# Order of the three part products, and VectorE's low parts of h one slot later, in a fused attention and expert layer

## The chip, the cores and the metric

One core of a Trainium2 chip runs the whole program. The metric is the device time of one execution in microseconds, lower is better. TensorE is called PE in the rows, its weight loads PEld, VectorE is DVE, ScalarE is ACT, GpSimd is POOL, and SyncE, whose queue issues the transfers, is SP.

## The reference

The input is 4 batches of 1024 tokens with 128 features. After a layer norm without weights, two branches run on the same tokens: 16-head attention with its own layer norm, and a mixture of 8 experts with a hidden size of 512, of which the best 2 are weighed per token. The result is the input plus attention times silu(experts).

```python
x = L0_attn_z
xn = _layernorm(x, axis=-1)
s = _L0_attn_ref(xn, ...)            # softmax(q k / sqrt(8)) v, 16 heads of 8, then W_proj
g = _silu(_L0_ffn_ref(xn, ...))
x = x + s * g

# in _L0_ffn_ref: all 8 experts are computed for every token
h = gelu(einsum('td,edh->eth', xf, W1) + b1[:, None, :], approximate=False)
expert_out = einsum('eth,ehd->etd', h, W2) + b2[:, None, :]
out = einsum('etd,te->td', expert_out, weights)
```

## The kernel before

The 4096 tokens are cut into NG = 8 groups of 512. The program has two stages. In the **expert stage** each group passes through HT = 32 chunks: 8 experts times 4 chunks of 128 hidden features. In the **attention stage** that follows, 32 pairs of heads are worked off in 256 blocks. The change touches only the expert stage.

**Products in parts.** A product in full fp32 costs several passes on TensorE, so most are made from rounded parts in fp32r. A weight matrix w is held as a high part (`w1h`, `w2h`, tile `w_hi`) and a low part (`w1l`, `w2l`, tile `w_lo`); the activations likewise: `xh`, `xl` (tiles `xn_t_hi`, `xn_t_lo`) and `hh`, `hl` (tiles `h_hi`, `h_lo`). `up(i)` makes the hidden chunk i from three products into one PSUM bank: L947 high by high, L948 low weights by high x, L949 high weights by low x. `down(i)` adds the chunk into the expert's output by three products as well: L968 and L969 with `hh`, and L971 with `hl`. Every fourth chunk (i = 3 mod 4) is not split and goes through L963 in fp32. Each product loads its own weights (a PEld row beside the PE row).

**Who makes h.** ScalarE takes the bank of `up(i)` twice through gelu: L823 writes the rounded `hh`, L826 the full `h_split` (`h32`). The low part is `h_split - h_hi`. VectorE makes it for the first chunk of each expert (i = 0 mod 4, `by_vector`, line L1272), GpSimd for the next two (L685). `down(i)` waits for it in `hl_done`, just ahead of L971.

**The order.** Every engine works off a plan of slots, one slot per chunk, that is written out by hand; `run_slots` calls the steps of slot 0, 1, 2, ... in order. Within a slot of group g stand first what is left of the experts of group g-1, then the extras, then the preparation of group g+1 (`pre`: statistics, router, q, k and v), then the experts of group g. TensorE runs `up(i)` in slot i and `down(i)` in slot i+3. The extras are the **early row maxima** for the attention stage: TensorE's product L985 writes one of two banks in turn, VectorE's L1336 reduces it. Product m waits until maximum m-2 is done, because it writes the same bank (`early_scores`, `pe.wait_ge(S("R"), m - 1)`). There are 256 of them, 27 in each 32 slots, so some slots hold two.

**VectorE's queue is strictly in order.** In slot i it holds, as far as present: the maxima, the preparation step, `low_h(i)` or `combine(e)` (L1289, in slots 4e+7). Its low part begins with `wait(dve, "h32", ...)`, and everything behind it on VectorE stands until ScalarE has written `h_split`.

## Time and profile before

| | us |
|---|---|
| median of 3 runs | 1103.75 (1102.54 to 1105.91) |
| the profiled execution | 1103.0 |
| its span, first to last instruction | 1101.2 |
| of this the expert stage | to about 512 |
| of this the attention stage | from about 512 |

The profiled execution is 0.75 us below the median; 1.8 us of it lie outside the span. In the steady part of the expert stage one group of 512 tokens takes about 62 us: VectorE's first low part of a group starts at 272.53, 334.80, 396.56 and 457.72 us. In the 60 us from 300 to 360 us TensorE is busy for 58.33 us, VectorE for 47.66, ScalarE for 41.42, GpSimd for 39.09, at the full TensorE clock (2.4 GHz).

A matmul's row is longer than the time that it holds up the next one: its end is modelled. An fp32r product of 512 columns is shown with 0.39 us, while the next one starts 0.23 us later. So a wait of TensorE costs the time between two starts minus 0.23 us, which is 0.16 us more than the idle time that is shown in brackets behind the row.

### The profile page before, as it was taken

The page shows a single profiled execution, that of the slowest core. Times are in us where ns is not written, and L with a number is a line of the kernel's source. Part 1 is how long each engine was busy: PE and PEld are TensorE (multiplying, and loading weights), DVE is VectorE, ACT ScalarE, POOL GpSimd, SP SyncE. Part 2 cuts the span into 40 slices and gives each one's busy share as a digit, 9 for nine tenths or more (in the row PEclk, how much of TensorE's full clock was granted, in tenths as well). Part 3 has the DMA queues.
Part 4 walks back from the last instruction along what each step waited for, and adds up shares of the span by engine and source line. Part 5 has one row for each costly group of instructions (what it writes and reads, how often), then busy time and mean ns, then how long its engine had stood idle before and what let it go on. Part 6 is the DMA issues. An engine that isn't in the chain of part 4 may idle for free.

```text
span 1101.2 us, 17451 instructions
## 1 busy us (share of the span) xinstructions
PE 1029.3 (93%) x5865; PEld 444.1 (40%) x5897; DVE 883.7 (80%) x1589; ACT 866.9 (79%) x1190; POOL 368.0 (33%) x555
## 2 busy tenths in 40 slices
PE   4998999999999999999999999999999999999997
PEld 3675666666666666664222222122222121122222
DVE  5647877787878787765999899989998998899943
ACT  6876667676767677666898998989898989798985
POOL 4786656657666667554001000001000001000010
PEclk9999999999999999999999999999999999999998
DMA  6432221414142232324212221212112221122102
GB/s 183 123 99 68 66 83 31 120 30 121 31 107 50 64 80 51 97 51 120 51 44 53 55 53 39 68 40 54 42 52 51 56 53 42 51 53 54 25 24 82
DMA packets 99410, 72.02 MB, mean 65 GB/s; under 512 B 21693, under 2 KB 83834, under 8 KB 99322
## 3 DMA queue, kind: packets, MB, share of 16 engines
q1 hardware_dynamic: 99322, 70.92, 24.5%
q8 instruction: 47, 0.77, 0.3%
q14 instruction: 41, 0.34, 0.1%
HBM read 53.12 MB, written 15.46 MB: 62 GB/s over the span
## 4 chain that ended last, share of the span: by engine, by line
PE 34%; ACT 8%; DVE 7%; issue 2%; SPq 1%; DMA 0%; POOL 0%; ACTq 0%; DVEq 0%; POOLq 0%
PE psum L1055 17%; PE psum L1034 8%; ACT p_ring L869 8%; PE psum L999 7%; DVE neg_max_half L1318 7%; PE psum L1084 1%; ACT o_sb L860 1%; DMA den<-o_sb 0%; SPq L469 0%; PE psum L1098 0%; PE psum L1010 0%; SPq L473 0%; DVE neg_max_rest L1327 0%; DVE y L1379 0%; POOL h_lo L685 0%
## 5 line engine op out<-in xcount | busy, mean ns | idle before, releaser
L869 ACT ACTIVATE p_ring<-psum 128x1024 f32<-128x1024 f32 x512 | 494.8, 1026 | 59.7 <-PE psum L1034 54.3
L1318 DVE TENSOR_REDUCE neg_max_half<-psum 128x1 f32<-128x512 f32 x768 | 481.6, 681 | 44.5 <-PE psum L999 36.7
L1055 PE MATMUL psum<-p_ring,v_sb 128*9 128x512 f32 x2048 | 269.2, 598 | 0.4 <-ACT o_sb L860 0.3
L823 ACT ACTIVATE h_hi<-psum,cols 128x512 fp32r<-128x512 f32 x192 | 132.4, 690 | 132.2 <-PE psum L949 131.2
L999 PE MATMUL psum<-k_max_stack,q_max_stack 48*128 48x512 bf16 x768 | 202.2, 380 | 16.6 <-DVE neg_max_half L1318 16.3
L1336 DVE TENSOR_REDUCE neg_max_half<-psum 128x1 f32<-128x512 f32 x256 | 169.3, 683 | 51.7 <-PE psum L985 45.0
L685 POOL TENSOR_TENSOR h_lo<-h_split,h_hi 128x512 fp32r<-128x512 f32 x128 | 165.1, 1294 | 135.4 <-ACT h_split L826 135.2
L1034 PE MATMUL psum<-q_stack,k_stack 51*128 51x512 bf16 x1024 | 200.0, 386 | 3.4 <-ACT p_ring L869 2.2
L635 POOL CAST neg_max_parts<-neg_max_rest 128x16 bf16<-128x16 f32 x32 | 6.3, 197 | 493.6 <-DVE neg_max_rest L1327 493.5
L1034 PEld LDWEIGHTS psum<-q_stack,k_stack 51*128 51x128 bf16 x1024 | 49.5, 93 | 299.2 <-ACT p_ring L869 276.2
L947 PE MATMUL psum<-xn_t_hi,w_hi 128*128 128x512 f32 x256 | 144.8, 566 | 0.7 <-DVE neg_max_half L1336 0.5
L826 ACT ACTIVATE h_split<-psum,cols 128x512 f32<-128x512 f32 x192 | 131.5, 685 | 0.0
L949 PE MATMUL psum<-xn_t_lo,w_hi 128*128 128x512 f32 x256 | 102.6, 401 | 0.0
L948 PE MATMUL psum<-xn_t_hi,w_lo 128*128 128x512 f32 x256 | 101.8, 398 | 0.0
L1272 DVE TENSOR_TENSOR h_lo<-h_split,h_hi 128x512 fp32r<-128x512 f32 x64 | 56.8, 888 | 51.9 <-ACT h_split L826 51.8
L985 PE MATMUL psum<-k_max_stack,q_max_stack 128*128 128x512 bf16 x224 | 82.9, 387 | 13.1 <-DVE neg_max_half L1336 12.2
L971 PE MATMUL psum<-h_lo,w_hi 128*128 128x512 f32 x192 | 77.5, 403 | 5.1 <-POOL h_lo L685 2.8
L968 PE MATMUL psum<-h_hi,w_hi 128*128 128x512 f32 x192 | 76.8, 400 | 0.0
L969 PE MATMUL psum<-h_hi,w_lo 128*128 128x512 f32 x192 | 76.1, 396 | 0.0
L999 PEld LDWEIGHTS psum<-k_max_stack,q_max_stack 48*128 48x128 bf16 x768 | 52.4, 94 | 55.6 <-DVE neg_max_half L1318 49.2
L676 POOL TENSOR_TENSOR acc<-acc,prod 128x512 f32<-128x512 f32 x48 | 64.9, 1352 | 12.2 <-DVE prod L1289 12.0
L963 PE MATMUL psum<-h_full,w_full 128*128 128x512 f32 x128 | 65.4, 592 | 0.0
(129 smaller groups left out, 957.5 us busy)
## 6 DMA issues: line engine op xcount, KB each, us to landing
expert_w_bc<-expert_w_dram SPq DMA_DIRECT2D x64, 256.0 KB, 5.1
k_rows_dram<-qk_parts SPq DMA_DIRECT2D x24, 256.0 KB, 3.1
q_max_stack<-q_rows_dram SPq DMA_DIRECT2D x64, 96.0 KB, 2.5
k_max_stack<-k_rows_dram SPq DMA_DIRECT2D x64, 96.0 KB, 2.5
q_stack<-q_rows_dram SPq DMA_DIRECT2D x64, 96.0 KB, 2.4
k_stack<-k_rows_dram SPq DMA_DIRECT2D x64, 96.0 KB, 2.5
q_rows_dram<-qk_parts SPq DMA_DIRECT2D x8, 384.0 KB, 2.6
xz<-in_L_attn_z_dram SPq DMA_DIRECT2D x8, 256.0 KB, 3.2
```

What stands on the lines that cost most here:

```text
L685: pool.tensor_tensor(hl[:, (g * HS + j) % HR, :], h32[:, (g * HS + j) % FR, :], hh[:, (g * HS + j) % HR, :].bitcast(F32), ALU.subtract)\
L823: act.activation(hh[:, (g * HS + j) % HR, :], up, ACT.Gelu, bias=col(C_B1 + i))\
L826: act.activation(h32[:, (g * HS + j) % FR, :], up, ACT.Gelu, bias=col(C_B1 + i))\
L869: act.activation(p_sb[:, n % PR, a, :, :].rearrange("p h t -> p (h t)"), scores_bank[s % 2], ACT.Exp, scale=SCALE).then_inc(S("P"), 1)
L947: pe.matmul(o, w1h[:, e, ws], G(xh, g), start=True, stop=False)
L948: pe.matmul(o, w1l[:, e, ws], G(xh, g), start=False, stop=False)
L949: pe.matmul(o, w1h[:, e, ws], G(xl, g), start=False, stop=True).then_inc(S("h"), 1)
L999: pe.matmul(ring_bank(("max", u))[:, :], q_m[rows, p % 2, t * P:(t + 1) * P], k_m[rows, p % 2, hh, c * TG:(c + 1) * TG], start=True, stop= ...
L1034: i = pe.matmul(scores_bank[s % 2][:, hh * TG:(hh + 1) * TG], k_s[rows, slot, kt * P:(kt + 1) * P], q_s[rows, slot, a * TG:(a + 1) * TG], ...
L1055: i = pe.matmul(o_bank[at:at + VR, :], v_sb[:, b * KT + kt, 2 * (p % PB) + hh, :], p_sb[:, n % PR, a, hh, :], start=(kt == 0), stop=(kt == ...
L1318: dve.tensor_reduce(mx[:, p % MXR, c, hh * NT + t:hh * NT + t + 1], ring_bank(("max", u)), AX.X, ALU.max, negate=True).then_inc(S("R"), 1)
L1336: dve.tensor_reduce(mx[:, p % MXR, c, hh * NT + t:hh * NT + t + 1], early_bank[m % 2], AX.X, ALU.max, negate=True).then_inc(S("R"), 1)
```

## The change

Two edits of TensorE's lines swap the order of two products, so that the one with the low weights comes first and the two that read the same high weights stand behind each other. One edit of VectorE's plan puts its low part of h into the next slot.

```diff
@@ up(i)
-                        pe.matmul(o, w1h[:, e, ws], G(xh, g), start=True, stop=False)
-                        pe.matmul(o, w1l[:, e, ws], G(xh, g), start=False, stop=False)
+                        pe.matmul(o, w1l[:, e, ws], G(xh, g), start=True, stop=False)
+                        pe.matmul(o, w1h[:, e, ws], G(xh, g), start=False, stop=False)
                         pe.matmul(o, w1h[:, e, ws], G(xl, g), start=False, stop=True).then_inc(S("h"), 1)
@@ down(i)
-                        pe.matmul(o, w2h[:, e, ws], hh[:, at, :], start=(c == 0), stop=False)
-                        pe.matmul(o, w2l[:, e, ws], hh[:, at, :], start=False, stop=False)
+                        pe.matmul(o, w2l[:, e, ws], hh[:, at, :], start=(c == 0), stop=False)
+                        pe.matmul(o, w2h[:, e, ws], hh[:, at, :], start=False, stop=False)
                         hl_done(pe, g, i)
                         pe.matmul(o, w2h[:, e, ws], hl[:, at, :], start=False, stop=False).then_inc(S("m2"), 1)
@@ VectorE's experts(g)
                 for i in range(HT):
                     if split(i) and by_vector(i):
-                        plan.setdefault(i, []).append(low_h(i))
+                        plan.setdefault(i + 1, []).append(low_h(i))
```

TensorE has as many instructions after as before. In what follows L947 and L968 name the first product of the three, whatever it reads. Place P, one chunk in the middle of the expert stage on TensorE, before:

```order
L947 MATMUL psum<-xn_t_hi,w_hi 128x512
L948 MATMUL psum<-xn_t_hi,w_lo 128x512
L949 MATMUL psum<-xn_t_lo,w_hi 128x512
L968 MATMUL psum<-h_hi,w_hi 128x512
L969 MATMUL psum<-h_hi,w_lo 128x512
L971 MATMUL psum<-h_lo,w_hi 128x512
```

The same place P after:

```order
L947 MATMUL psum<-xn_t_hi,w_lo 128x512
L948 MATMUL psum<-xn_t_hi,w_hi 128x512
L949 MATMUL psum<-xn_t_lo,w_hi 128x512
L968 MATMUL psum<-h_hi,w_lo 128x512
L969 MATMUL psum<-h_hi,w_hi 128x512
L971 MATMUL psum<-h_lo,w_hi 128x512
```

Only the weights of the first two products of each three change places; the moving operands keep their order.

Place A on VectorE, slots 19 to 23 of a group with the router's last step (L1241) ahead, before:

```order
289 L1241 TENSOR_TENSOR router<-router,router_sum 128x32
290 L1289 SCALAR_TENSOR_TENSOR prod<-psum,cols,expert_w_bc 128x512
291 L1336 TENSOR_REDUCE neg_max_half<-psum 128x1
292 L1272 TENSOR_TENSOR h_lo<-h_split,h_hi 128x512
293 L1336 TENSOR_REDUCE neg_max_half<-psum 128x1 x3
294 L1327 TENSOR_TENSOR neg_max_rest<-neg_max_half 128x16
```

Place A after:

```order
292 L1241 TENSOR_TENSOR router<-router,router_sum 128x32
293 L1289 SCALAR_TENSOR_TENSOR prod<-psum,cols,expert_w_bc 128x512
294 L1336 TENSOR_REDUCE neg_max_half<-psum 128x1 x3
295 L1272 TENSOR_TENSOR h_lo<-h_split,h_hi 128x512
296 L1336 TENSOR_REDUCE neg_max_half<-psum 128x1
297 L1327 TENSOR_TENSOR neg_max_rest<-neg_max_half 128x16
```

The two maxima of slot 21 stand ahead of the low part of chunk 20 instead of behind it.

Place B on VectorE, slots 7 to 10, behind the second guess of the layer norm (L1163), before:

```order
334 L1163 TENSOR_SCALAR newton<-guess 128x4
335 L1289 SCALAR_TENSOR_TENSOR acc<-psum,cols,expert_w_bc 128x512
336 L1336 TENSOR_REDUCE neg_max_half<-psum 128x1
337 L1272 TENSOR_TENSOR h_lo<-h_split,h_hi 128x512
338 L1336 TENSOR_REDUCE neg_max_half<-psum 128x1 x4
```

Place B after:

```order
339 L1163 TENSOR_SCALAR newton<-guess 128x4
340 L1289 SCALAR_TENSOR_TENSOR acc<-psum,cols,expert_w_bc 128x512
341 L1336 TENSOR_REDUCE neg_max_half<-psum 128x1 x2
342 L1272 TENSOR_TENSOR h_lo<-h_split,h_hi 128x512
343 L1336 TENSOR_REDUCE neg_max_half<-psum 128x1 x3
```

One maximum more stands ahead of the low part of chunk 8.

## Rows read from the trace of the kernel before

**Rows 1.** The page: busy time of each engine with its share.
```profile
PE 1029.3 (93%) x5865; PEld 444.1 (40%) x5897; DVE 883.7 (80%) x1589; ACT 866.9 (79%) x1190; POOL 368.0 (33%) x555
```

**Rows 2.** Busy time by stretch: PE, PEld, DVE, ACT, POOL, clock, DMA share, GB/s.
```profile
300.00:360.00 60.00, 58.33 (x244) 39.09 (x248) 47.66 (x91) 41.42 (x74) 39.09 (x59) 1.00 0.29 74
```

**Rows 3.** Waits of PE from 60 to 500 us: us, times, longest.
```profile
PE psum L985 <- DVE neg_max_half L1336: 12.2, 17, 1.9
```

**Rows 4.** Waits of DVE in the same stretch.
```profile
DVE h_lo L1272 <- ACT h_split L826: 44.8, 45, 2.8
```

**Rows 5.** In order of time (start, length): fp32r products with one weight load each.
```profile
284.26 0.39 PE L948 MATMUL psum<-xn_t_hi,w_lo 128*128 128x512 f32 x1
284.49 0.40 PE L949 MATMUL psum<-xn_t_lo,w_hi 128*128 128x512 f32 x1
```

**Rows 6.** Weight loads by line, 60 to 430 us: busy, mean ns.
```profile
L949 PEld LDWEIGHTS psum<-xn_t_lo,w_hi 128*128 128x128 f32 x190 | 35.9, 189 | 8.2
L985 PEld LDWEIGHTS psum<-k_max_stack,q_max_stack 128*128 128x128 bf16 x209 | 19.3, 97 | 65.2 <-issue 33.6 <-DVE neg_max_half L1336 31.4
L963 PEld LDWEIGHTS psum<-h_full,w_full 128*128 128x128 f32 x96 | 18.1, 188 | 4.2
```

**Rows 7.** Place A in order of time, all engines.
```profile
247.93 0.61 PE L985 MATMUL psum<-k_max_stack,q_max_stack 128*128 128x512 bf16 x2
...
248.70 1.18 POOL L614 TENSOR_TENSOR qk_full<-qk_full,qk_parts 128x512 f32<-128x512 f32 x1
...
248.73 1.70 DVE L1272 TENSOR_TENSOR h_lo<-h_split,h_hi 128x512 fp32r<-128x512 f32 x1 [0.75 <-ACT h_split L826]
...
250.35 1.87 DVE L1336 TENSOR_REDUCE neg_max_half<-psum 128x1 f32<-128x512 f32 x3
251.08 0.39 PE L985 MATMUL psum<-k_max_stack,q_max_stack 128*128 128x512 bf16 x1 [1.04 <-DVE neg_max_half L1336]
251.09 1.28 POOL L685 TENSOR_TENSOR h_lo<-h_split,h_hi 128x512 fp32r<-128x512 f32 x1 [1.21 <-ACT h_split L826]
...
252.90 0.58 PE L947 MATMUL psum<-xn_t_hi,w_hi 128*128 128x512 f32 x1
```

**Rows 8.** The last of the four waits of place A.
```profile
436.44 0.39 PE L985 MATMUL psum<-k_max_stack,q_max_stack 128*128 128x512 bf16 x1 [1.02 <-DVE neg_max_half L1336]
```

**Rows 9.** Place B in order of time.
```profile
287.28 0.68 DVE L1272 TENSOR_TENSOR h_lo<-h_split,h_hi 128x512 fp32r<-128x512 f32 x1
...
287.88 1.88 DVE L1336 TENSOR_REDUCE neg_max_half<-psum 128x1 f32<-128x512 f32 x3
288.62 0.39 PE L985 MATMUL psum<-k_max_stack,q_max_stack 128*128 128x512 bf16 x1 [0.73 <-DVE neg_max_half L1336]
```

**Rows 10.** Smaller waits behind a low part, in order of time.
```profile
107.97 0.39 PE L985 MATMUL psum<-k_max_stack,q_max_stack 128*128 128x512 bf16 x1 [0.40 <-DVE neg_max_half L1336]
...
342.67 0.39 PE L985 MATMUL psum<-k_max_stack,q_max_stack 128*128 128x512 bf16 x1 [0.15 <-DVE neg_max_half L1336]
```

**Rows 11.** The start of a group: low part of chunk 0 and its product.
```profile
396.56 0.69 DVE L1272 TENSOR_TENSOR h_lo<-h_split,h_hi 128x512 fp32r<-128x512 f32 x1 [0.73 <-ACT h_split L826]
...
397.77 0.67 DVE L1186 BATCH_NORM_STATS2 bn_parts<-xz 128x6 f32<-128x128 f32 x3
...
399.83 0.40 PE L971 MATMUL psum<-h_lo,w_hi 128*128 128x512 f32 x1
```

**Rows 12.** The start of the second group, where x lands late.
```profile
84.89 0.67 DVE L1272 TENSOR_TENSOR h_lo<-h_split,h_hi 128x512 fp32r<-128x512 f32 x1
...
85.61 0.80 PE L971 MATMUL psum<-h_lo,w_hi 128*128 128x512 f32 x1 [2.35 <-DVE h_lo L1272]
```

**Rows 13.** A long wait whose maximum stands ahead of the low part.
```profile
159.27 0.68 DVE L1336 TENSOR_REDUCE neg_max_half<-psum 128x1 f32<-128x512 f32 x1
...
160.01 0.39 PE L985 MATMUL psum<-k_max_stack,q_max_stack 128*128 128x512 bf16 x1 [1.89 <-DVE neg_max_half L1336]
```

**Rows 14.** Durations of L1272, ns: least, median, most.
```profile
L1272 DVE TENSOR_TENSOR h_lo<-h_split,h_hi x64: 673/693/1696, 17.1 to 505.9; 128x512 fp32r<-128x512 f32 x64
```

## The prediction

> **What bounds the kernel now.** The busy times come first [rows 1]: TensorE at 93%, VectorE at 80%, ScalarE at 79%. That is a mean over two stages, and only the expert stage is changed, so the next view is the busy time by stretch [rows 2]. Of 60 us TensorE is busy for 58.33 at full clock, VectorE for 47.66. TensorE sets the pace, and the question is where its remaining gaps are. The waits of TensorE from 60 to 500 us answer it [rows 3]: 12.2 us in 17 waits of L985, the early product, for a row maximum of VectorE, and once it waits for a low part of h, 2.35 us [rows 12]. Against this stands VectorE's own idle time [rows 4]: 44.8 us in 45 waits, in which a low part of h is at the head of its queue and ScalarE has not yet written the operand. VectorE is not short of time; it stands in front of a closed door while maxima queue behind it that TensorE will soon want. The order in time shows the link at two places [rows 7, 9].
>
> **The swap of products on TensorE.** It removes no instruction: each of the 256 `up` and 192 `down` steps keeps three products and three loads. An fp32r product starts 0.23 us after the one before [rows 5]. The load is 189 ns [rows 6], so it is nearly as long as the step. No row of before shows two fp32r products in turn on the same weights, so the price of this is bounded. The dear end is 0: a step is as long as one full load allows, and no row shows a longer one at this clock without a wait. The cheap end: if the repeated load cost nothing, the step would be that of a product with a short load. The two bf16 products with loads of 97 ns [rows 6] start 0.61 - 0.39 = 0.22 us apart [rows 7], so 0.01 us for each of 448 repeats, 4.5 us. The nearest row is L963: its two records per product read the same fp32 weights, and each shows a load of its own of 188 ns [rows 6], 96 loads for 48 products. A repeated load is made in full there. I take 0.
>
> The Trainium skill (TensorE: Matmul & The Clock Gate, Part 2, step 1) says that loading is apart from multiplying so that weights can be loaded once and used for many products, which speaks for a gain from this pairing; the same page (Back-to-back issue gap) gives N/2.4 + 2.5 ns between warm products, 216 ns for 512 columns. By it the sum would fall by 448 x 14 ns = 6.3 us, an estimate, if the load were dropped. The trace does not bear it out as far as it goes: L963 loads the same weights twice.
>
> The semaphores are not touched: `w_lo` is waited for before all three products, and L971, the only one that waits for the low part of h, stays last.
>
> **The low part one slot later on VectorE.** No instruction is added here either; 64 subtractions of some 0.69 us [rows 14] move behind the maxima of the next slot. What goes are TensorE's waits for a maximum that stood directly behind a low part. I went through them in order of time. Each is the distance of two starts less 0.23 us, thus 0.16 us more than the idle time shown.
>
> Place A, the low part of chunk 20 [rows 7]. VectorE idles 0.75 us for ScalarE up to 248.73, then the low part takes 1.70 us, and the next maximum starts at 250.35, ends at about 251.0, and TensorE goes on at 251.08 after 1.04 us of idleness. The two products that these maxima read had started at 247.93 and 248.15, so after the change the maxima run from about 248.3 to 249.6, and TensorE finds them done. ScalarE is next in line: chunk 21 was ready at 251.08, when GpSimd took it up, and TensorE's up(23), which needs it, would start at 252.90 - 1.19 = 251.7; 0.6 us are left. So 1.04 + 0.16 = 1.2 us go, and this wait stands in four groups (251.08, 313.33, 375.11, 436.44) with 1.02 to 1.04 us [rows 7, 8]: 4 x 1.19 = 4.8 us.
>
> Place B, the low part of chunk 8 [rows 9]. Here VectorE does not idle: low part and maximum follow each other 0.60 us apart, and TensorE waits 0.73 us for the second maximum. It moves ahead by one step of 0.60 us. The same 0.60 us at 226.35, 288.62 and 404.44: 1.8 us.
>
> Smaller ones [rows 10]: 107.97, behind a low part that had to wait for ScalarE, 0.40 + 0.16 = 0.56 us; 280.40 and 342.67, where low part, sum and maximum follow each other, 0.15 + 0.16 = 0.31 each; 463.97 (0.43, by way of GpSimd), 459.07 (0.14), 465.98 (0.33) and 486.59 (0.30). Together 0.56 + 0.62 + 1.20 = 2.4 us.
>
> What does not go: the longest waits, as at 160.01 with 1.89 us [rows 13], end with a maximum that stands ahead of the low part, behind the guess of the layer norm.
>
> What is added: the low part comes later, and L971 is queued behind it on TensorE. By the order of time the product follows the end of the low part by 2.57 us at least in the groups from 130 us on, and by 3 to 5 us in most places. The tightest is the start of a group [rows 11]: low part ends at 397.25, product at 399.83. After the change one maximum (0.60) and three statistics (0.6) stand ahead of it, 1.2 us, or 1.8 with two maxima: it is hidden. One place has no cover: at 84.89 the first statistic has waited for x, the low part follows it at once, and TensorE stands for it [rows 12]. There three statistics, 0.6 us as a group [rows 11], come in between, and TensorE goes on 0.6 us later: +0.6 us.
>
> The steps that are moved past are maxima and preparation; none of them waits for the low part, and VectorE issues no DMA. SP's and GpSimd's queues keep their order.
>
> The sum: 4.8 + 1.8 + 2.4 - 0.6 = 8.4 us. One deduction: around place B VectorE runs without a gap for some 6 us, so it may well owe the moved 0.6 us to the next product; I take off half of B's 1.8 us, 0.9 us, and 0.1 for rounding. That leaves 7.4 us: 1103.0 - 7.4 = 1095.6 for the profiled execution, and with its 0.75 us below the median 1096.3 as the forecast.
>
> **Rivals.**
> *The gain is given back.* TensorE arrives 1.2 us earlier at the next thing that VectorE, ScalarE or GpSimd must finish, and waits there instead. For it: ScalarE's spare time at place A is only 0.6 us, and the waits behind the layer norm's guess [rows 13] hang on a chain through GpSimd that does not get faster. Against it: VectorE waited for ScalarE, thus for TensorE, in 45 of 64 low parts [rows 4], so it is early elsewhere. If two thirds are lost: 1103.75 - 2.5 = 1101.2, between 1100.5 and 1103.75.
>
> *The repeated load is cheaper.* Then 4.5 us more: 1096.3 - 4.5 = 1091.8. The rows on L963 speak against it.
>
> *The low part runs into GpSimd and the kernel gets slower.* L1272 takes 0.68 us alone and up to 1.70 [rows 14]; in the long cases GpSimd is reading at the same time: its L614 runs from 248.70 to 249.88 and the low part ends 0.55 us after it [rows 7]. GpSimd starts its own subtraction for the next chunk as soon as ScalarE has written that, about 1.9 us after the operand of VectorE's low part. If the low part starts later than those 1.9 us, it stands for up to 1.28 us [rows 7] with the next maximum behind it, and TensorE waits for that. If this met two places in each of 7 groups with 1.0 us each, it would be +14 us, less 8.4: 1103.75 + 5.6 = 1109.4. At place A the low part would start at 249.6, 0.9 us after its operand, and GpSimd's L685 at 251.09: the point is not reached there. In slots 17 and 25, where router or q and k steps also stand ahead, it may be.
>
> The Trainium skill (SBUF — State Buffer, on the shared port pair) states this as an exclusive lock: a VectorE operation with two SBUF inputs and a GpSimd operation that reads SBUF exclude each other, and the later one blocks until the first is done. By that rule the trace agrees: 1.70 against 0.68 us.
>
> **How the numbers follow.** The forecast, a gain of 4 to 10 us, has 0.60. Given back: 0.22. Cheaper load: 0.06. Slower: 0.08. The remaining 0.04 is a change that does nothing measurable. A measurement of this kernel can tell about 0.3%, 3.3 us, from no change. Faster by more: 0.60 + 0.06 and a small part of the second case, 0.68. Within: 0.22. Slower by more: 0.10. The range goes from 1091.0, just below the cheaper load, to 1103.0, near no change; this leaves out the slower case and the edges of the others, 2 in 10.
>
> **What would show it.** In the profile of the changed kernel: TensorE's waits for maxima fall from 12.2 us in 17 waits to some 5 us, and the four waits of over 1 us at place A are gone. VectorE's idle time ahead of L1272 falls from 44.8 us to under 20. Between fp32r products the step stays at 0.23 us, with as many loads as products. The waits behind the layer norm's guess stay. The attention stage has the same length and only starts earlier. I am wrong if L971 waits for L1272 in more than one or two places, if the step falls to 0.22 us, if L1272's mean rises, or if the waits of L985 keep their sum at other places.

## The result and the profile after

The kernel with both edits takes 1095.96 us (median of 4 runs, 1093.71 to 1096.51), against 1104.38 us of before beside it (4 runs, 1102.54 to 1105.91). The ratio is 0.9928 [0.9907, 0.995], a gain of 7.9 us, between 5.5 and 10.3. A second measurement with more runs (below) gave 0.9946 [0.9924, 0.9968]. The forecast was 1096.3 us, faster. One of the 11 runs of before beside the last three experiments was slow, 1435.66 us at a granted clock of 0.66, and is left out of their ratios.

The profiled execution took 1093.71 us, with a span of 1091.9 us. This is the fastest of its runs, so the two traces lie 9.3 us apart, a little more than the medians do. Where the difference lies is told by the start of the attention stage: its first L1034 starts at 512.7 us before and at 505.4 us after. So the expert stage is 7.3 us shorter. The rest of the program takes 588.5 us before and 586.6 after; over all thirteen traces it lies between 586.4 and 590.0. What orders it is the clock and not the change: in six traces the granted clock stands near half for some 3 to 7 us about 425 us into the attention stage (in before from 938.5 us on, 0.57 from 938 to 942), and their rest takes 588.2 to 590.0 us; in the other seven, after among them, it does not, and the rest takes 586.4 to 588.1. `move_only`, which makes the move, is one of the six, and `same_weights`, which does not, is one of the seven. So these 1.9 us are not put down to the change.

First the page of after, which answers to [rows 1].

```profile
span 1091.9 us, 17483 instructions
PE 1028.1 (94%) x5897; PEld 443.5 (41%) x5897; DVE 886.7 (81%) x1589; ACT 865.9 (79%) x1190; POOL 370.7 (34%) x555
```

No engine has less work; TensorE's record count differs only by the 32 records that are missing in before. The change can only be seen in the waits. These are the waits from 60 to 500 us, which answer to [rows 3, 4] (us in total, times, longest).

```profile
DVE neg_max_half L1336 <- PE psum L985: 80.7, 118, 2.4
...
PE psum L985 <- DVE neg_max_half L1336: 6.1, 11, 1.9
DVE h_lo L1272 <- ACT h_split L826: 4.6, 3, 2.0
...
PE psum L971 <- DVE h_lo L1272: 3.0, 1, 3.0
```

TensorE's waits for a maximum have halved, from 12.2 us in 17 waits to 6.1 us in 11. VectorE's idle time in front of a low part has nearly gone, from 44.8 us to 4.6 us. VectorE is not busier for that: it now waits in front of the maxima, for TensorE (80.7 us; 43.9 us before), which is where a helper of the bounding engine should wait.

Place A in order of time, to be laid beside [rows 7].

```profile
245.69 0.61 PE L985 MATMUL psum<-k_max_stack,q_max_stack 128*128 128x512 bf16 x2
...
246.18 1.29 DVE L1336 TENSOR_REDUCE neg_max_half<-psum 128x1 f32<-128x512 f32 x2 [0.45 <-PE psum L985]
246.45 1.17 POOL L614 TENSOR_TENSOR qk_full<-qk_full,qk_parts 128x512 f32<-128x512 f32 x1
...
247.39 0.78 DVE L1272 TENSOR_TENSOR h_lo<-h_split,h_hi 128x512 fp32r<-128x512 f32 x1
...
247.64 0.39 PE L985 MATMUL psum<-k_max_stack,q_max_stack 128*128 128x512 bf16 x1
```

The two maxima start 0.49 us after their products, the low part follows them, and its operand has long been there. The next early product, at 247.64, waits for nothing; in before it stood for 1.04 us. The low part also nearly escapes GpSimd's L614: 0.78 us instead of 1.70.

Place B, to be laid beside [rows 9].

```profile
283.80 0.68 DVE L1336 TENSOR_REDUCE neg_max_half<-psum 128x1 f32<-128x512 f32 x1
...
284.40 0.68 DVE L1272 TENSOR_TENSOR h_lo<-h_split,h_hi 128x512 fp32r<-128x512 f32 x1
...
284.54 0.39 PE L985 MATMUL psum<-k_max_stack,q_max_stack 128*128 128x512 bf16 x1 [0.21 <-DVE neg_max_half L1336]
```

The wait has shrunk from 0.73 to 0.21 us, by nearly the length of the low part.

**The account by group.** The first L963 of each group is a good milestone, since it is a record of TensorE at the same step of each group's order. The rows of before (the first two) and of after (the last two) show one such interval.

```profile
281.32 1.02 PE L963 MATMUL psum<-h_full,w_full 128*128 128x512 f32 x2
343.59 1.02 PE L963 MATMUL psum<-h_full,w_full 128*128 128x512 f32 x2
```

```profile
277.59 1.02 PE L963 MATMUL psum<-h_full,w_full 128*128 128x512 f32 x2
338.01 1.02 PE L963 MATMUL psum<-h_full,w_full 128*128 128x512 f32 x2
```

The table has all intervals, in us. "Foretold" is what the forecast's steps say for that interval, before the deduction of 1.0 us.

| from L963 to the next, before | length before | after | difference | foretold |
|---|---|---|---|---|
| start to 91.74 (after: to 92.99) | 91.74 | 92.99 | +1.25 | +0.60 |
| to 153.64 | 61.90 | 60.59 | -1.31 | -0.56 |
| to 218.78 | 65.14 | 63.60 | -1.54 | 0 |
| to 281.32 | 62.54 | 60.41 | -2.13 | -2.10 |
| to 343.59 | 62.27 | 60.42 | -1.85 | -2.10 |
| to 405.36 | 61.77 | 60.32 | -1.45 | -1.79 |
| to 466.90 | 61.54 | 61.83 | +0.29 | -2.09 |
| to 512.73, the first L1034 | 45.83 | 45.21 | -0.62 | -0.30 |
| sum | 512.73 | 505.37 | -7.36 | -8.34 |

The sum is close to the forecast's 7.4 us. It is so in part by luck, because errors of both signs meet and because 1.5 us of it are a matter of the clock: four lines, the first three and the seventh, stand 0.6 us or more from what was foretold, and the section on the steps takes them up.

The next two fences, of after, show two of them. This is the seventh group, with two waits that before does not have.

```profile
400.52 1.23 DVE L1154 TENSOR_TENSOR newton<-mean_var,newton 128x4 f32<-128x4 f32 x1
...
401.79 1.22 DVE L1156 TENSOR_TENSOR newton<-newton 128x4 f32<-128x4 f32 x1
...
405.08 0.39 PE L985 MATMUL psum<-k_max_stack,q_max_stack 128*128 128x512 bf16 x1 [0.43 <-DVE neg_max_half L1336]
405.33 1.28 POOL L685 TENSOR_TENSOR h_lo<-h_split,h_hi 128x512 fp32r<-128x512 f32 x1 [1.24 <-ACT h_split L826]
405.53 1.63 DVE L1272 TENSOR_TENSOR h_lo<-h_split,h_hi 128x512 fp32r<-128x512 f32 x1
...
407.08 1.87 DVE L1336 TENSOR_REDUCE neg_max_half<-psum 128x1 f32<-128x512 f32 x3
407.82 0.39 PE L985 MATMUL psum<-k_max_stack,q_max_stack 128*128 128x512 bf16 x1 [0.60 <-DVE neg_max_half L1336]
```

GpSimd's subtraction starts 0.20 us ahead of VectorE's, and VectorE's then takes 1.63 us instead of 0.68. The maxima stand behind it, and TensorE waits for them at 407.82. This is the third rival of the forecast, in one place. The wait at 405.08 comes before that low part and is another matter: it follows VectorE's two operations on the variance (L1154, L1156), which take over 1.2 us each. With 0.16 us on each, as the forecast counts waits, the two waits cost 0.59 and 0.76 us, together 1.35.

And this is the start of the second group, which answers to [rows 12].

```profile
85.36 0.87 DVE L1186 BATCH_NORM_STATS2 bn_parts<-xz 128x6 f32<-128x128 f32 x4 [7.76 <-DMA xz<-in_L_attn_z_dram]
86.15 0.68 DVE L1272 TENSOR_TENSOR h_lo<-h_split,h_hi 128x512 fp32r<-128x512 f32 x1
...
86.88 0.79 PE L971 MATMUL psum<-h_lo,w_hi 128*128 128x512 f32 x1 [3.04 <-DVE h_lo L1272]
```

All four statistics now stand between the late x and the low part, and TensorE stands for it. L971 starts 1.27 us later than in before.

### The profile page after: what moved, and what is told of

It is laid out like the page before. It is cut to its first block, busy times and chain, and to the rows that moved or that the text cites. A ratio compares the mean times of both kernels' runs of the same rounds, so it can differ in the third digit from the quotient of the medians.

```text
span 1091.9 us, 17483 instructions
## 1 busy us (share of the span) xinstructions
PE 1028.1 (94%) x5897; PEld 443.5 (41%) x5897; DVE 886.7 (81%) x1589; ACT 865.9 (79%) x1190; POOL 370.7 (34%) x555
## 4 chain that ended last, share of the span: by engine, by line
PE 35%; ACT 9%; DVE 7%; issue 2%; POOL 0%; ACTq 0%; DVEq 0%; POOLq 0%
PE psum L1055 17%; PE psum L1034 9%; ACT p_ring L869 8%; PE psum L999 7%; DVE neg_max_half L1318 7%; PE psum L1084 1%; ACT o_sb L860 0%; PE psum L1098 0%; PE psum L1010 0%; DVE neg_max_rest L1327 0%; DVE y L1379 0%; POOL h_lo L685 0%; PE psum L1090 0%; PE psum L963 0%; DVE rden L1358 0%
## 5 line engine op out<-in xcount | busy, mean ns | idle before, releaser
L1336 DVE TENSOR_REDUCE neg_max_half<-psum 128x1 f32<-128x512 f32 x256 | 171.5, 685 | 81.6 <-PE psum L985 80.7
L685 POOL TENSOR_TENSOR h_lo<-h_split,h_hi 128x512 fp32r<-128x512 f32 x128 | 166.1, 1302 | 125.6 <-ACT h_split L826 125.6
L1034 PE MATMUL psum<-q_stack,k_stack 51*128 51x512 bf16 x1024 | 200.5, 386 | 3.4 <-ACT p_ring L869 2.3
L1034 PEld LDWEIGHTS psum<-q_stack,k_stack 51*128 51x128 bf16 x1024 | 49.5, 93 | 298.5 <-ACT p_ring L869 278.8
L947 PE MATMUL psum<-xn_t_hi,w_lo 128*128 128x512 f32 x256 | 144.7, 565 | 0.3 <-ACT h_split L826 0.3
L948 PE MATMUL psum<-xn_t_hi,w_hi 128*128 128x512 f32 x256 | 101.6, 397 | 0.0
L985 PE MATMUL psum<-k_max_stack,q_max_stack 128*128 128x512 bf16 x256 | 94.0, 388 | 6.2 <-DVE neg_max_half L1336 6.1
L971 PE MATMUL psum<-h_lo,w_hi 128*128 128x512 f32 x192 | 77.4, 403 | 5.7 <-DVE h_lo L1272 3.0
L968 PE MATMUL psum<-h_hi,w_lo 128*128 128x512 f32 x192 | 76.3, 398 | 0.0
L969 PE MATMUL psum<-h_hi,w_hi 128*128 128x512 f32 x192 | 75.6, 394 | 0.0
L963 PE MATMUL psum<-h_full,w_full 128*128 128x512 f32 x128 | 65.9, 596 | 0.0
L1272 DVE TENSOR_TENSOR h_lo<-h_split,h_hi 128x512 fp32r<-128x512 f32 x64 | 56.6, 884 | 8.9 <-ACT h_split L826 8.9
```

What stands on the lines that cost most here:

```text
L685: pool.tensor_tensor(hl[:, (g * HS + j) % HR, :], h32[:, (g * HS + j) % FR, :], hh[:, (g * HS + j) % HR, :].bitcast(F32), ALU.subtract)\
L947: pe.matmul(o, w1l[:, e, ws], G(xh, g), start=True, stop=False)
L948: pe.matmul(o, w1h[:, e, ws], G(xh, g), start=False, stop=False)
L1034: i = pe.matmul(scores_bank[s % 2][:, hh * TG:(hh + 1) * TG], k_s[rows, slot, kt * P:(kt + 1) * P], q_s[rows, slot, a * TG:(a + 1) * TG], ...
L1336: dve.tensor_reduce(mx[:, p % MXR, c, hh * NT + t:hh * NT + t + 1], early_bank[m % 2], AX.X, ALU.max, negate=True).then_inc(S("R"), 1)
```

## The experiments

Each edit is shown against before unless it says otherwise. Ratios are to before, with the 95% interval.

### The two edits apart

`move_only` makes the edit on VectorE alone.

```diff
                 for i in range(HT):
                     if split(i) and by_vector(i):
-                        plan.setdefault(i, []).append(low_h(i))
+                        plan.setdefault(i + 1, []).append(low_h(i))
```

> Only VectorE's low part goes one slot later; the products keep the old order. Theory (the whole gain is the low part's new slot): ratio to before 0.992 to 0.993, the same as with both edits; waits of L985 for a maximum about 6 us instead of 12. Rival (the pairing of equal weights carries part of the gain, up to 4.5 us): ratio 0.996 or more.

Measured: 1095.35 us, ratio 0.9936 [0.9912, 0.996].

`swap_only` makes the two swaps on TensorE alone.

```diff
-                        pe.matmul(o, w1h[:, e, ws], G(xh, g), start=True, stop=False)
-                        pe.matmul(o, w1l[:, e, ws], G(xh, g), start=False, stop=False)
+                        pe.matmul(o, w1l[:, e, ws], G(xh, g), start=True, stop=False)
+                        pe.matmul(o, w1h[:, e, ws], G(xh, g), start=False, stop=False)
...
-                        pe.matmul(o, w2h[:, e, ws], hh[:, at, :], start=(c == 0), stop=False)
-                        pe.matmul(o, w2l[:, e, ws], hh[:, at, :], start=False, stop=False)
+                        pe.matmul(o, w2l[:, e, ws], hh[:, at, :], start=(c == 0), stop=False)
+                        pe.matmul(o, w2h[:, e, ws], hh[:, at, :], start=False, stop=False)
```

> Only the two products change places; the low part keeps its slot. Theory: no change, ratio 0.998 to 1.002, and the step from L968 to L969 to L971 stays at 0.23 us with a load of 189 ns each. Rival (repeated loads are cheaper, 0.01 us for each of 448): ratio 0.996 and a step of 0.22 us from the second to the third product.

Measured: 1102.95 us, ratio 1.0003 [0.9989, 1.0017]. Its profile in order of time, loads and products, at the pair with the same weights (start, length):

```profile
284.44 0.19 PEld L969 LDWEIGHTS psum<-h_hi,w_hi 128*128 128x128 f32 x1
284.68 0.39 PE L969 MATMUL psum<-h_hi,w_hi 128*128 128x512 f32 x1
284.68 0.19 PEld L971 LDWEIGHTS psum<-h_lo,w_hi 128*128 128x128 f32 x1
284.90 0.40 PE L971 MATMUL psum<-h_lo,w_hi 128*128 128x512 f32 x1
```

L971 uses the same weights as L969, and they are loaded again, in 0.19 us. The step is 0.22 us here and between 0.22 and 0.24 elsewhere, as between products whose weights differ.

`same_weights` drives this to the end: all three products of each step read the high weights, so the part of the low weights is left out of the result.

```diff
-                        pe.matmul(o, w1l[:, e, ws], G(xh, g), start=False, stop=False)
+                        pe.matmul(o, w1h[:, e, ws], G(xh, g), start=False, stop=False)
...
-                        pe.matmul(o, w2l[:, e, ws], hh[:, at, :], start=False, stop=False)
+                        pe.matmul(o, w2h[:, e, ws], hh[:, at, :], start=False, stop=False)
```

> The order of before, but all three products of a chunk read the same high weights, so that 896 loads repeat the one before instead of none. The part of the sum that the low weights bring is left out of the computation. Theory (a repeated load costs as much as a new one): ratio 0.998 to 1.002, all steps 0.23 us. Rival (a repeated load is cheaper, 0.01 us each): 9 us less, ratio 0.992.

Measured: 1102.91 us, ratio 1.0011 [0.9995, 1.0026]. Its products follow each other as in before:

```profile
284.84 0.40 PE L949 MATMUL psum<-xn_t_lo,w_hi 128*128 128x512 f32 x1
285.08 0.40 PE L968 MATMUL psum<-h_hi,w_hi 128*128 128x512 f32 x1
285.32 0.39 PE L969 MATMUL psum<-h_hi,w_hi 128*128 128x512 f32 x1
```

Even with twice as many pairs on the same weights nothing is gained: a repeated load costs what any other does. The rival of the cheaper load has fallen.

`both_edits_again` is the kernel after, unchanged, on the same chip as the three above.

> The changed kernel itself beside the others, on the same chip. Theory: ratio 0.992 to 0.994. It is the yardstick for the two halves: the low part alone should give the same ratio within 0.002.

Measured: 1096.13 us, ratio 0.9946 [0.9924, 0.9968]. It can't be told from the move alone. So the gain that can be measured is the move on VectorE, and the swap adds nothing to it. The clock does not carry the gain of both edits: the mean granted clock of the runs is 0.9887 with both edits and 0.9886 in before beside them (0.9898 in `move_only`, which may owe it a part of its gain).

### The move, taken apart by chunk

`only_chunk20` moves the low parts of chunk 20 alone, those of place A.

```diff
-                        plan.setdefault(i, []).append(low_h(i))
+                        plan.setdefault(i + (1 if i == 20 else 0), []).append(low_h(i))
```

> Of the eight low parts of a group only that of chunk 20 goes one slot later (place A). Theory: it carries the largest term, four waits of 1.2 us: 4.8 us, ratio 0.9957, and no wait of 1.0 us is left at 251, 313, 375 and 436 us. Rival (every low part that ends VectorE's idle time gives alike): one eighth of the gain, 1 us, ratio 0.999.

Measured: 1097.99 us, ratio 0.9964 [0.9951, 0.9976], a gain of 4.0 us (2.6 to 5.4). The milestones put its period at 61.04 us from 279.78 to 340.82, against 62.27 in before, and the two neighbours fall to 61.33 and 60.60, against 62.54 and 61.77. That is 1.2 us in each. Place A is worth what was foretold; over four groups it makes 4.8 us, within the interval.

`only_chunk8` moves those of place B alone.

```diff
-                        plan.setdefault(i, []).append(low_h(i))
+                        plan.setdefault(i + (1 if i == 8 else 0), []).append(low_h(i))
```

> Only the low part of chunk 8 goes one slot later (place B). Theory: 0.9 to 1.8 us less, ratio 0.9984 to 0.9992. VectorE has no idle time there, so the 0.6 us may be owed to the next product. Rival as before: 1 us, which can't be told from it; the waits of L985 at place B tell: 0.13 us instead of 0.73.

Measured: 1101.21 us, ratio 0.9996 [0.9982, 1.001]: the interval holds the expected gain and none. The trace says more. Its periods are 61.90, 61.65 and 61.76, so 0.64 and 0.62 us less in the groups of 226.35 and 288.62, and nothing in the group that holds 404.44. There the wait still stands, only earlier by the clock:

```profile
401.18 0.39 PE L985 MATMUL psum<-k_max_stack,q_max_stack 128*128 128x512 bf16 x1 [0.74 <-DVE neg_max_half L1336]
```

In before it is 0.73 us. This wait does not hang on chunk 8. It comes 1.96 us behind the low part that starts at 399.22 in this trace, that of chunk 4. In before the waits of 280.40, 342.67 and 404.44 all stand 0.92 us ahead of the first L963 of their group, so they are one place, behind chunk 4, and the waits of 226.35 and 288.62, over 7 us behind that L963, are another.

`all_but_8_and_20` moves the other six.

```diff
-                        plan.setdefault(i, []).append(low_h(i))
+                        plan.setdefault(i + (0 if i in (8, 20) else 1), []).append(low_h(i))
```

> The other six low parts of a group go one slot later, chunks 8 and 20 keep their slot. Theory: 2.4 us less from the smaller waits and 0.6 more at the second group: 1.8 us less, ratio 0.9984. Rival (every low part alike): 6 us less, ratio 0.9946.

Measured: 1099.83 us, ratio 0.9995 [0.998, 1.0009]: the interval holds the expected 0.9984 and no gain. Its milestones show both sides. The group from 343.98 to 404.89 is 60.91 us long, 0.86 less than in before: the wait of 404.44 is gone, so it is chunk 4 that carries it. The groups in the middle gain 0.35 and 0.06 us. The group behind it, from 404.89 to 467.11, is 0.67 us longer than in before, although chunk 8 keeps its slot, and a wait stands in it that before does not have:

```profile
411.63 0.39 PE L985 MATMUL psum<-k_max_stack,q_max_stack 128*128 128x512 bf16 x1 [0.42 <-DVE neg_max_half L1336]
```

It is the wait that after has at 405.08, 6.7 us behind the group's first L963 in both. Against the gains stands also the start of the second group, whose first L963 comes at 94.09 us instead of 91.74: chunk 0 is among the six. Not all of these 2.35 us are the edit's, since the granted clock stands at half for longer here (below).

### How far the low part can be moved

`two_slots_later` moves all by two slots.

```diff
-                        plan.setdefault(i, []).append(low_h(i))
+                        plan.setdefault(i + (2), []).append(low_h(i))
```

> All low parts go two slots later than before, one more than in the change. Theory: all the waits that one slot took away stay away, but the low part of chunk 0 now ends after its product wants it (1.8 us were left, one more slot is 1.8 to 1.9 us): L971 waits for L1272 at the start of six groups, up to 0.5 us each, so 1 to 4 us more than with one slot, ratio 0.995 to 0.998. Rival (GpSimd's own subtraction stands in the way from 1.9 us on): mean of L1272 over 1.1 us instead of 0.88, and a ratio over 1.000.

Measured: 1100.83 us, ratio 1.0002 [0.9988, 1.0017]. The gain of one slot is lost altogether. The theory gave it 0.995 to 0.998; the rival, with a mean of L1272 over 1.1 us and a ratio over 1.000, fits better: the mean is 1.13 us, against 0.88 in after. Durations of L1272 in ns (least, median, most), first in after, then with two slots:

```profile
L1272 DVE TENSOR_TENSOR h_lo<-h_split,h_hi x64: 672/682/1783, 17.4 to 498.6; 128x512 fp32r<-128x512 f32 x64
```

```profile
L1272 DVE TENSOR_TENSOR h_lo<-h_split,h_hi x64: 673/1032/1787, 22.5 to 503.1; 128x512 fp32r<-128x512 f32 x64
```

The median rises by a half, since with two slots 35 of the 64 low parts start when GpSimd is at its own subtraction, against 6 in after. A place in order of time, from the trace with two slots:

```profile
335.44 1.29 POOL L685 TENSOR_TENSOR h_lo<-h_split,h_hi 128x512 fp32r<-128x512 f32 x1 [3.10 <-ACT h_split L826]
...
335.78 1.50 DVE L1272 TENSOR_TENSOR h_lo<-h_split,h_hi 128x512 fp32r<-128x512 f32 x1
...
337.33 0.50 PE L971 MATMUL psum<-h_lo,w_hi 128*128 128x512 f32 x1
```

The low part starts 0.34 us behind GpSimd's and is held until that has ended at 336.73. TensorE's L971 at 337.33 starts right behind its end: the cover that one slot leaves here is used up. The trace is still 1.3 us shorter from 281.83 to 342.77, where place A is, but its first L963 of the third group comes at 155.87 instead of 153.64, and the ratio, over 12 runs, sees no gain. The traced run is the fastest of the twelve, 1098.48 us, so the trace shows more gain than the kernel has, and what the others lose is not shown.

### Two waits that the change leaves or makes

These are edits of the kernel after, and they aim at its two longest waits, the 3.04 us at 86.88 and the 1.89 us at 159.95. `x_later` puts the statistics of x behind the low part of chunk 0.

```diff
-                return {0: [x_here, spread(0, 1)], 1: [spread(1, 4)], 3: [moments, guess_rsqrt(g, 1)],
+                return {2: [x_here, spread(0, 4)], 3: [moments, guess_rsqrt(g, 1)],
```

> The changed kernel, and in the preparation all four statistics of x stand in slot 2 (before: one in slot 0, three in slot 1), thus behind the low part of chunk 0. Theory (L971's wait of 3.0 us at the second group is VectorE standing for x with the low part behind it): that wait goes, and the stretch at half clock behind it with it: 3 to 4 us less than the changed kernel, ratio to before 0.990 to 0.991. Rival (the preparation of the group, which the late x holds up, is what TensorE waits for next): the wait turns up at L985 or at the transposes, and the ratio stays at 0.994.

Measured: 1094.29 us, ratio 0.9932 [0.9918, 0.9946], as the rival had it. The wait is gone at L971, and another stands in its place:

```profile
85.08 0.87 DVE L1186 BATCH_NORM_STATS2 bn_parts<-xz 128x6 f32<-128x128 f32 x4 [3.97 <-DMA xz<-in_L_attn_z_dram]
...
88.29 0.61 PE L985 MATMUL psum<-k_max_stack,q_max_stack 128*128 128x512 bf16 x1 [2.88 <-DVE neg_max_half L1336]
```

x lands at much the same time, 85.08 us against 85.36, and whatever VectorE does next in its order waits for it, now the maxima. The first L963 of the group comes at 92.99 us in both. Only an x that arrives earlier would help; that was not tried.

`v_on_gpsimd` has GpSimd, which has the reciprocal root already, make the three small operations on the variance, so that VectorE's stand-still beside GpSimd's subtractions at 155 to 158 us would go.

```diff
+                        ch.sync()
+                        pool.tensor_tensor(nwt[:, 5, :], nwt[:, 6, :], y, ALU.mult).then_inc(S("nwt"), 1)
+                        v = nwt[:, 0, :]
+                        ch.mark(pool.tensor_tensor(v, mv[:, :, 1], y, ALU.mult))
+                        ch.sync()
+                        ch.mark(pool.tensor_tensor(v, v, y, ALU.mult))
                         ch.end()
-                        pool.tensor_tensor(nwt[:, 5, :], nwt[:, 6, :], y, ALU.mult).then_inc(S("nwt"), 1)
+                        pool.tensor_scalar(v, v, EPS, None, ALU.add).then_inc(S("v2"), 1)
...
-                    else:
+                    elif not g:
                         wait(dve, "nwt", g, 2, 1)
...
+                    else:
+                        wait(dve, "v2", g, 1, 0)
```

> The changed kernel, and GpSimd makes the second variance (L1154, L1156, L1158) right behind its own Newton steps, for all groups but the first. Theory (the longest waits left, 2.06 us at 160 us and 0.2 to 1.1 in the other groups, come from these two small VectorE operations, which take up to 1.2 us each while GpSimd reads): 3 to 5 us less than the changed kernel, ratio 0.990 to 0.991. Rival (GpSimd gets 0.9 us more per group and its low parts come late): L971 waits for L685, ratio 0.994 or more.

Measured: 1094.73 us, ratio 0.9938 [0.9924, 0.9952], no more than both edits give. First the place in after:

```profile
155.36 2.54 POOL L685 TENSOR_TENSOR h_lo<-h_split,h_hi 128x512 fp32r<-128x512 f32 x2
...
155.46 1.20 DVE L1154 TENSOR_TENSOR newton<-mean_var,newton 128x4 f32<-128x4 f32 x1
...
156.69 1.23 DVE L1156 TENSOR_TENSOR newton<-newton 128x4 f32<-128x4 f32 x1
```

The same place in this kernel, whose lines stand further down (L691 is L685, L1168 and L1171 are the shift and the subtraction of the guess, L991 is the early product):

```profile
155.99 2.53 POOL L691 TENSOR_TENSOR h_lo<-h_split,h_hi 128x512 fp32r<-128x512 f32 x2
156.06 1.25 DVE L1168 TENSOR_SCALAR guess<-newton 128x4 int32<-128x4 int32 x1 [0.65 <-POOL newton L670]
...
157.42 1.13 DVE L1171 TENSOR_SCALAR newton<-guess 128x4 int32<-128x4 int32 x1
...
159.85 0.39 PE L991 MATMUL psum<-k_max_stack,q_max_stack 128*128 128x512 bf16 x1 [1.77 <-DVE neg_max_half L1344]
```

The products that were held are gone from VectorE, and the next two operations are held in their stead. TensorE's wait goes from 1.89 to 1.77 us. In the seventh group the edit does help: the two waits of 405.08 and 407.82 are gone, one of 0.21 us for GpSimd's low part has come, and the group takes 61.01 us instead of 61.83.

`x_later_v_on_gpsimd` has both edits together.

> Both of these on top of the changed kernel. Theory: the savings add up, 6 to 9 us less than the changed kernel, ratio 0.986 to 0.989. Rival: the same chain ends last in both, and the second one brings nothing: ratio 0.990 to 0.991.

Measured: 1092.55 us, ratio 0.9919 [0.9903, 0.9935]. It is the fastest of all by its median. Its interval overlaps with those of `x_later`, of `v_on_gpsimd` and of both edits, and neither edit removed the long wait it was made for, so I don't call it a gain over the kernel after.

## Why the prediction was right, step by step

**The swap at nothing: right.** 1.0003 alone and 1.0011 with all products on the same weights. The Trainium skill (TensorE: Matmul & The Clock Gate, Part 2, step 1) speaks of one load for many products; 6.3 us less, the forecast's estimate from that page's issue gap, are outside the interval of `swap_only`, whose lower end is 1.2 us less. On this path each product is issued with its own load, and the rows show that the repeated one is made in full.

**Place A, 4.8 us: right.** The three waits at 251.08, 313.33 and 375.11 us are gone; alone they give 1.2 us per group. The fourth, at 436.44, is gone as well: the stretch between two L963 around it falls from 8.15 us (429.21 to 437.36) to 6.97 us (423.54 to 430.51). But its group as a whole gains nothing, for the reason that follows.

**Place B, 1.8 us less a deduction of 0.9: right in sum, wrong in both parts.** The deduction was not needed. VectorE did not owe the time to the next product: the period falls by 0.6 us in both groups. And the wait at 404.44 was put down to the wrong low part. It is the place of the small waits at 280.40 and 342.67, behind chunk 4, and the forecast took it for place B because it is as long; chunk 8 alone leaves it as it is.

**The seventh group: the step that failed.** Foretold were 2.09 us less, and it became 0.29 us longer. Two new waits at its start cost 1.35 us, and they have two causes.

The second, at 407.82, stands where the low part of chunk 8 meets GpSimd's subtraction. The forecast had this as the rival that slows the kernel, "in slots 17 and 25", with the condition that the low part starts later than 1.9 us behind its operand. It happened at slot 9, in this group alone, in `after`, `both_edits_again`, `move_only` and `x_later`. The low part starts 1.63 us behind its operand, which ScalarE had written at 403.90, but the operand of chunk 9 came 1.35 us behind that of chunk 8, and not 1.9.

The first, at 405.08, is the rival of the gain given back. With the wait of 404.44 gone, TensorE comes earlier to a maximum that stands behind VectorE's operations on the variance, which take 1.23 and 1.22 us while GpSimd's two subtractions run from 400.45 to 402.99, and 0.16 us each where GpSimd leaves them alone (7.82 us in after). `all_but_8_and_20` has the same wait with chunk 8 in its old slot, and `v_on_gpsimd`, where VectorE does not make these operations, has neither of the two. In `only_chunk20`, where chunks 4 and 8 stand still, the same group is 60.37 us long, 1.17 less than in before.

And the wait for GpSimd at the group's end grew:

```profile
457.33 0.24 PE L1010 MATMUL psum<-ident_b,neg_max_parts 128*48 128x128 bf16 x1 [0.68 <-POOL neg_max_parts L641]
```

It is 0.36 us in before, at 463.97; the forecast had it gone, for 0.43 us. It is 0.68 us in `all_but_8_and_20` as well and 0.35 in `only_chunk20` and `only_chunk8`, so it hangs on another low part than those two. With 1.35 us for the new waits and 0.75 for this one, 0.28 us of the 2.38 have no row.

**The smaller waits, 2.4 us: partly.** Those of 107.97, 280.40 and 342.67 are gone. Not foretold is that the wait of 97.59 (1.38 us) falls to 0.89, and the one of 151.14 (0.46 us) to 0.15, so the group up to 153.64 gains 1.31 us instead of 0.56.

**The start of the second group, 0.6 us: right, but a cost ahead of it was not seen.** L971 starts 1.27 us later than in before. The three statistics account for 0.6 us, as foretold. The rest comes from the first group: x lands 0.68 us later in after (85.36 against 84.68), and its transfer seems to follow TensorE's progress, since over the traces x comes late where TensorE is late. TensorE was 0.55 us late by then, at the L963 of 75.79 against 75.24. 0.13 us of that were there at the L963 of 69.62, and 0.42 arise here, in after:

```profile
68.29 1.77 DVE L1272 TENSOR_TENSOR h_lo<-h_split,h_hi 128x512 fp32r<-128x512 f32 x1
...
73.42 1.28 POOL L685 TENSOR_TENSOR h_lo<-h_split,h_hi 128x512 fp32r<-128x512 f32 x1
...
74.76 0.50 PE L971 MATMUL psum<-h_lo,w_hi 128*128 128x512 f32 x1 [0.16 <-POOL h_lo L685]
```

VectorE's and GpSimd's subtractions hold each other, GpSimd's at 73.42 is 0.59 us later than the one at 72.83 in before, and its product has to wait. From the L963 at 69.62 to that at 75.79 it is 6.17 us, against 5.75 in before. The 0.42 us stand in all the traces in which every low part, or all but chunks 8 and 20, is moved (6.15 to 6.19), and in none of the others, `swap_only`, `same_weights`, `only_chunk20` and `only_chunk8` (5.74 to 5.75). This is the third rival again, with GpSimd as the one that is held.

**The group up to 153.64 also has the clock.** Behind the wait at the second group's start the granted clock falls: in before it is 0.50 in the stretch from 86 to 88 us and 0.84 from 88 to 90, in after 0.61 and 0.53. In `all_but_8_and_20` it is 0.50 up to 92 us; in `only_chunk20`, with a wait of 2.23 us, it stays at 1.00 until the milestone, which comes at 90.44, and falls to 0.50 at 98 us, behind a wait of 1.90 us. So one to three microseconds around this place differ from trace to trace with it, and a term of 0.6 us can't be read off two traces here.

**1.5 us that no step has.** From 153.64 to 218.78 the forecast has nothing, and the trace is 1.54 us shorter. The rows show what it is (the columns are those of [rows 2]). First before, then after, both behind the same wait of 1.89 us at 160 us:

```profile
160.00:162.00 2.00, 1.99 (x8) 1.78 (x9) 1.75 (x3) 0.00 (x0) 0.00 (x0) 0.58 0.28 68
162.00:164.00 2.00, 2.00 (x7) 1.26 (x6) 0.00 (x0) 1.46 (x3) 0.12 (x1) 0.57 0.27 63
```

```profile
160.00:162.00 2.00, 2.00 (x11) 1.53 (x11) 1.68 (x3) 0.49 (x1) 0.00 (x0) 1.00 0.29 72
162.00:164.00 2.00, 2.00 (x9) 1.25 (x8) 0.69 (x1) 2.00 (x5) 1.15 (x1) 1.00 0.21 59
```

In before the clock falls to near its lower level, 1.2 GHz, for some 3 us. In after it does not. `swap_only` and `all_but_8_and_20` show the drop and 65.2 us; `same_weights`, which moves nothing, shows none and 63.6 us, as do `only_chunk20` and `only_chunk8`. So the move is not needed for it, and I don't count it as the change's. Without these 1.5 us the expert stage is 5.8 us shorter, not 7.4. `same_weights` is the fairer trace to lay beside after, since its low parts keep their old slot and it has no drop here: its attention stage starts at 511.0 us, 5.6 us later. So the forecast's steps gave some three quarters of their sum in the trace; the ratios, which give 5.9 to 7.9 us, can't tell 5.6 from 7.4. Whether the move makes the drop rarer is open: it stands in three of the six traces in which not all low parts are moved and in none of the seven in which all are.

**The rival of the gain given back: small.** TensorE did not come to new waits for ScalarE. It gave back 0.59 us to VectorE's operations on the variance in the seventh group. What the third rival took, 0.76 us there and 0.42 in the first, went to GpSimd.

**The signs.** They came: 6.1 us against "some 5", four waits of over 1 us gone, VectorE's idle time at 4.6 us against "under 20", the step unchanged. Of the signs of being wrong none came: L971 waits for L1272 in one place, as in before, and L1272's mean is 0.88 us, against 0.89. (The 45 waits of [rows 4] are from 60 to 500 us, where 58 low parts stand; the forecast set them against all 64.) The guess's wait stays at 1.89 us to the hundredth. And the attention stage kept its length but for the 1.9 us that go with the clock.

## What to carry to other kernels

An in-order engine with free time can still hold up the one that sets the pace: look for its idle time in front of an operation whose operand is late, and at what is queued behind it; moving that operation behind the urgent ones takes no further instruction and gave 0.5 to 0.7% here. Moving it further is not better, since one slot gave 7 us and two gave none: the operation meets another engine's work, and its own consumer comes near. When a sum of small terms comes out right, lay a milestone in each period and compare period by period, since here +2.4 us and -1.5 us that nobody had foretold lay under a sum that fitted.

## What the runs showed of the hardware that I had not expected

**Small operations with one input are held by GpSimd too.** I had expected only VectorE operations with two inputs to be held. In `v_on_gpsimd` a shift and a subtraction with a constant on 128x4 elements take 1.25 and 1.13 us while GpSimd's two subtractions run from 155.99 to 158.52, and 0.17 us where GpSimd does not run (158.16 us in after). The Trainium skill (SBUF — State Buffer, SBUF: two separate sides) names two kinds of VectorE operation that exclude GpSimd, those with two SBUF inputs against a GpSimd operation that reads SBUF, and those in a two-port mode, and says that the later one waits for the whole of the other. By that rule the trace agrees, if these operations ran in such a mode, which no run here shows. Between the two subtractions of GpSimd the operation that was held gets through, in `v_on_gpsimd` with a short one right behind it (L1169, 0.16 us at 157.23), and the next of the chain is held by the second subtraction. So such a chain moves on by about one step per subtraction, some 1.25 us each.

**A wait of about 2 us may or may not bring the clock down.** Behind the wait of 1.8 to 1.9 us at 160 us the granted clock fell to about 0.57 for some 3 us in three traces and stayed at 1.00 in ten; behind that of 2.1 to 3.2 us at the second group's start it fell in twelve of the thirteen traces. Where it fell at 160 us the group was 1.5 us longer, so such a wait can cost nearly twice its length.
